# Sparse attention with RWKV feed-forward: batch 1's last six heads in groups of four and two instead of three and three

## The reference

```python
scores = jnp.einsum('bhqd,bhkd->bhqk', q, k) * scale
sparsity = scores.max(axis=-1) - scores.mean(axis=-1)
_, top_idx = jax.lax.top_k(sparsity, U)             # U = 307 of 4096
q_sel = jnp.take_along_axis(q, top_idx[..., None], axis=2)
attn = jax.nn.softmax(jnp.einsum('bhud,bhkd->bhuk', q_sel, k) * scale, axis=-1)
out_sel = jnp.einsum('bhuk,bhkd->bhud', attn, v)
out = jnp.zeros_like(q).at[bi, hi, top_idx].set(out_sel)
```

## Time and profile before

| | |
|---|---|
| median of three runs | 3249.06 us |
| profiled execution: time | 3248.58 us |
| profiled execution: span | 3246.8 us |
| mean granted TensorE clock | 0.981 of full speed |
| scoring pass: first and last reduction | 62.0 to 2953.2 us |
| group 7 selected, group 6 attended further | 2953.2 to 3028.0 us |
| group 7 attended | 3028.0 to 3080.4 us |
| feed-forward of batch 1 | from about 3091.7 us to the end |

### The profile page before, as it was taken

How to read it: one execution, slowest core, us unless ns; L and a number is a source line. 1 busy time by engine, 2 the same in 40 slices (tenths; PEclk the granted TensorE clock), 3 DMA queues, 4 the chain that set the end, 5 groups by cost and what they waited for, 6 DMA issues and landing times. The chain is left out here.

```text
span 3246.8 us, 56302 instructions
## 1 busy us (share of the span) xinstructions
PE 2943.3 (91%) x14620; PEld 1335.6 (41%) x14620; DVE 2878.9 (89%) x5704; ACT 2832.5 (87%) x6246; POOL 1608.3 (50%) x2867
## 2 busy tenths in 40 slices
PE   6999899998999999999899999899998899997587
PEld 3333333333433343343334454444444443343376
DVE  4999999999889998998999899899999898997567
ACT  5999898998999999899899888799988799896476
POOL 4223022224645553754355474766556663667654
PEclk8999999999999999999999999999999999999789
DMA  6334223352151123124121244212161115102122
GB/s 189 85 87 122 74 70 83 89 38 40 34 35 34 35 41 15 35 41 35 21 45 30 56 52 36 50 36 41 37 48 41 37 29 37 34 15 16 16 86 72
DMA packets 263597, 163.46 MB, mean 50 GB/s; under 512 B 168876, under 2 KB 242796, under 8 KB 259180
## 3 DMA queue, kind: packets, MB, share of 16 engines
q1 hardware_dynamic: 255180, 156.41, 27.6%
q0 software_dynamic: 6144, 1.37, 0.6%
q10 hardware_dynamic: 1952, 2.10, 0.2%
HBM read 111.86 MB, written 47.86 MB: 49 GB/s over the span
## 5 line engine op out<-in xcount | busy, mean ns | idle before, releaser
L1193 DVE CUSTOM_DVE_ANT_0 JK<-DP,AB 128x1024 bf16<-128x1024 f32 x2048 | 2462.7, 1222 | 228.8 <-DVE SPr L1193 87.1
L1037 ACT ACTIVATE AB<-CP 128x512 f32<-128x512 f32 x4096 | 2291.6, 623 | 186.3 <-PE CP L775 125.1
L794 PE MATMUL DP<-KS,QS 128*128 128x512 f16 x4096 | 1230.0, 382 | 58.0 <-DVE SPr L1193 51.0
L1681 POOL TENSOR_TENSOR SCR<-E 128x307 f16<-128x307 f32 x957 | 664.6, 707 | 485.2 <-ACT E L1072 479.0
L775 PE MATMUL CP<-KS,QS 128*128 128x512 f16 x2048 | 789.9, 386 | 54.1 <-ACT AB L1037 31.5
L784 PE MATMUL CP<-KS,QS 128*128 128x512 f16 x2048 | 790.5, 386 | 35.3 <-ACT AB L1037 0.6
L794 PEld LDWEIGHTS DP<-KS,QS 128*128 128x128 f16 x4096 | 355.4, 99 | 353.0 <-DVE SPr L1193 166.1
L1072 ACT ACTIVATE E<-BP 128x307 f32<-128x307 f32 x906 | 432.5, 477 | 37.9 <-PE BP L864 33.8
L775 PEld LDWEIGHTS CP<-KS,QS 128*128 128x128 f16 x2048 | 197.5, 96 | 525.7 <-ACT AB L1037 450.7
L784 PEld LDWEIGHTS CP<-KS,QS 128*128 128x128 f16 x2048 | 196.5, 96 | 417.0 <-ACT AB L1037 368.0
L864 PE MATMUL BP<-QT,KA 128*128 128x307 f16 x906 | 268.1, 296 | 23.5 <-ACT QT L1064 19.6
(11 more groups left out here) (421 smaller groups left out, 3044.5 us busy)
## 6 DMA issues: line engine op xcount, KB each, us to landing
KS<-KTC SPq DMA_DIRECT2D x256, 128.0 KB
QS<-QSC SPq DMA_DIRECT2D x512, 64.0 KB
KA<-KTC SPq DMA_DIRECT2D x128, 128.0 KB
QN<-SCR SPq DMA_DIRECT2D x16, 544.0 KB, 3.4
SCR<-in_L_attn_x SPq DMA_DIRECT2D x16, 512.0 KB, 5.1
AO<-E SPq DMA_DIRECT2D x16, 512.0 KB, 7.2
VF<-in_L_attn_x SPq DMA_DIRECT2D x64, 128.0 KB, 2.2
VF<-AO SPq DMA_DIRECT2D x64, 128.0 KB, 2.2
```

The costliest lines, as they stand in the source:

```text
L794: r = pe.matmul(o[:, 512 * j:512 * j + 512], qs, ks[j][:, 0, :], start=True, stop=True)
L1037: act.activation(AB[p % 3][:, 512 * j:512 * j + 512], BANK["C%d" % j], ACT.Abs).then_inc(ab_full, 1)
L1193: dve.tensor_tensor_reduce(out=JK[p % 2][:], in0=BANK["D%d" % u], in1=AB[p % 3][:], scale=1.0, scalar=0.0, op0=ALU.add, op1=ALU.max, accum ...
L1681: pool.tensor_tensor(EL[a % NE], E[a % NE][:], EH[a % NE], ALU.subtract).then_inc(el_g, 1)
```

## The change

One line. Group 6 of the list takes four heads of batch 1 (10 to 13, in all heads 26 to 29), group 7 takes two (14 and 15, in all heads 30 and 31).

```diff
-GROUPS = [(0, 0, 5), (0, 5, 5), (0, 10, 3), (0, 13, 3), (1, 0, 5), (1, 5, 5), (1, 10, 3), (1, 13, 3)]
+GROUPS = [(0, 0, 5), (0, 5, 5), (0, 10, 3), (0, 13, 3), (1, 0, 5), (1, 5, 5), (1, 10, 4), (1, 14, 2)]
```

## The result

The changed kernel takes 3264.58 us (median of 7 runs, 3260.79 to 3266.28), the kernel before beside it 3253.18 us (7 runs, 3247.30 to 3254.71). The ratio is 1.0037, 95% interval 1.0028 to 1.0046: slower by 0.37%, some 12 us. The profiled execution took 3266.28 us (span 3264.5), 17.7 us more than that of before.

What follows compares the result with a forecast made beforehand. The prediction took POOL, not PE, to be the engine in the chain of B and C; scoring pass -4.5, A +5, B +4, C +3.6, D +2.4 gave +10.5 on 3248.6, so 3259.1 us, range 3245 to 3270.

Steps and rivals of the forecast that it cites:

- A: Bit search of group 7 after the scoring pass, 42.3 us before: an added gather and arrangement interrupt POOL, +5 us.
- B: Cut, ranks, slots and one-hot tables, 19.2 us before: 17 tiles' subtractions and a gather join POOL's work, +4 us.
- C: Indices to HBM and back, gather, arrangement: group 7's gather starts later behind POOL's queue, +3.6 us, ends 0 and 5.
- D: Attention tiles after the arrangement, 108 instead of 96: 4.8 us more, less restart and boundary, +2.4 us, ends 0 and 5.
- Scoring pass: Up to the last scoring reduction: 33 tiles and one head's setup leave, selection gets wider; -4.5 us, ends -7 and -2.
- The price of a tile beside it: In the scoring pass an attention tile is nearly free, 0.17 us each, so 33 fewer save 5.6 us.
- the order shifted by hand: Head 31: selection ready at step 47, no tile in steps 9 to 46, then 17 tiles before the tail.
- The price of one interruption: In the bit search, an interruption of POOL by DMA issues costs the chain 4.5 us after it is over.
- The second view: POOL's own work to the arrangement's end is 78 us in a stretch of 73, so A to C cost at least +5.
- the gap filled cleanly: Rival, chance 0.13: tiles fill B and C within POOL's idle time, PE clock high; faster, 3241.3 us.
- POOL's work alone: Rival, chance 0.27: idle time closes up and no DVE operation starves; no change, 3251 us.
- The third rival: Chance 0.20: every POOL interruption starves the DVE, three more of 4.5 us in A and B; +20, 3268.6 us.

Runs made afterwards that it cites:

- the late start: Kernel before, three and three heads kept, with group 6's attention begun 36 scoring steps later, so 17 tiles in the pass and 175 after: 3265.44 us, ratio 1.0045.
- the run with the DVE in its place: Changed kernel with residual subtractions of group 6's third head (head 28) on the DVE from tile 17 on: 3254.70 us, ratio to before 1.0020.

## Why the prediction was right, and which step was not

- **The direction and the size**: 3259.1 us with 3245 to 3270 was forecast, 3264.58 measured; slower held. By the ratio the change cost 12 us, by the two profiled executions 17.7, and the sum said 10.5. That the sum comes so near the ratio is in part luck: A was put 3.5 us too high, which hides a part of what B, C and D were put too low.
- **Scoring pass, -4.5**: the pass ends 4.6 us earlier, but heads 28 to 31, which scatter far less than its end, give -6.5 us, near the far end of the range (-7 to -2). The price of a tile beside it held (0.17 us forecast, 0.19 with the late start), and so did the order shifted by hand: 38 bare steps (49.7 us, 51.6 forecast), 17 tiles. Of the 6.5 us 1.4 lie in head 28, for which no gain was forecast; it is 84.4 to 84.5 us in all traces of the changed order and 85.8 to 85.9 in all of the old one.
- **A, +5**: +1.5. The price of one interruption was right (5.3 us of idle time on the DVE behind head 28's gather). Wrong was that the interruption of before would stay: behind the put L1251 took 0.75 us for 4.75. It was over before the first subtraction began; what set that timing no experiment shows. The mechanism differs from the one foreseen too: not a DVE instruction that takes long, but the search's matmul standing on PE behind a product that waits for POOL.
- **B, +4**: +6.5, and 4.7, 4.8 and 5.8 in the other three traces with this order. Here the starved operation came (3.98 us against 0.22; 1.35 in two of the traces), as did the put ahead of the tables. With the subtractions taken off POOL the sum is back at 0.21 us. The value was a little low, the bounds (-1 and 8.5) held.
- **C, +3.6**: +5.5, half a microsecond over its upper end. The queue was as foretold, down to its seven subtractions and the arrangement. That no tile could go on behind it was said too, and the run with the DVE in its place shows what it cost: 7.0 us of C and D.
- **D, +2.4**: +9.3 here, 6.9 in the other trace with the same D; its upper end was 5. **This is the step that failed.** It counted 12 tiles at the steady pace of 0.40 us of Exp and let a boundary "take part of the rest". The runs show three things in its place. The group boundary, in the bare stretch before, now lies in the chain behind a put in POOL's queue: 7.9 us from product to product, 4.1 us of D when the tiles leave POOL. Second, the steady pace was too low a price: a whole D costs 54.2/96 = 0.56 us a tile before and 0.58 with groups of two and four, so 12 tiles are about 7 us, not 4.8. Third, the restart of 1.8 us that was to fall away did (the product after the arrangement's end starts 0.7 us behind it). 6.9 + 4.1 - 1.8 = 9.2 us, an estimate, against the 9.3 and 6.9 measured.
- **The second view**, POOL's own work as a floor of +5 us for A to C, held: +13.5, with +12.6 forecast by the parts.
- **The rivals**: the gap filled cleanly is refuted; it was filled, and at a clock of 0.71 and 0.70, not 1.0, so PE's clock in B came back only part of the way (0.67 and 0.50 before). POOL's work alone falls short by the starved sum. The third rival, where every interruption starves the DVE, put the time at 3268.6 us and is nearer to the median (4.0 us off) than the forecast is (5.5). As a change, +20 against +10.5, it is the farther from the 12 us of the ratio; but its three further starved operations were one (the sum in B) and one idle stretch in A, and the remainder came from D.

The running sum agrees with what the Trainium skill states on the page "SBUF — State Buffer", section "Who interferes with whom": a DVE instruction with two SBUF inputs contends with a GpSimd instruction that reads SBUF. It goes beyond that page in length: by the page's section "Summary: rules for kernel authors" the second to issue waits until the first finishes, and here the sum ended with the last of six subtractions in a row (3.98 us), 0.66 us from start to start.

## What to carry to other kernels

Before work is moved into a bare stretch of a chain, list what the engine in that chain has queued, issue of DMAs included, and give the price of every tile behind it: here POOL, not the idle PE, decided, and a tile placed in the gap cost as much as one behind it. Taking one waiting instruction off a crowded in-order engine only hands the wait to the next one; the whole run of them has to go, and then the gap is really filled (74 matmuls in C for 36, 7 us). When groups are resized, ask first what starts later, since 33 tiles that lose their cover cost more than a shorter pass gives back; a boundary between groups deserves a term of its own. And before one trace's stage is put down to a change, look at the same stage in other executions with the same order: B moved by 1.8 us and D by 2.4 with nothing edited in them.

## What was not expected of the hardware

- A DVE operation with two inputs in SBUF can wait out a run of subtractions on POOL: 3.98 us for six, 4.02 in another kernel and 4.75 for seven, where it takes 0.21 to 0.26 us without them. In these cases it ends within 0.11 us of the end of a subtraction. Yet it doesn't always wait for the whole run: the same sum took 1.35 us, two subtractions, in two traces with the same order, and most L1251 in the search stay under 0.8 us, one subtraction. What decides how many it waits for stays open.
- Three indirect DMA issues hold POOL's in-order queue for 3.7 us in B and 4.2 us at the group boundary (1.02, 1.18 and 1.36 us each, 0.30 between them).
- The granted clock of a stretch filled with attention was 0.71 and 0.70 (B and C), little above the 0.63 of B with nothing in it: here tiles that stopped and started behind POOL didn't bring the clock to 1.0.
